# A vision-tower kernel on one Trainium2 core: pixels loaded by half patches, and three engines' orders rearranged

## What is computed

```python
# patches of 16x16 pixels, 3 channels: 36 patches per image, 768 numbers each
p = x.reshape(B, C, nh, PH, nw, PW).transpose(0, 2, 4, 3, 5, 1).reshape(B, 36, 768)
h = layernorm(p, ln1) @ W + b            # 768 -> 192
h = layernorm(h, ln2)
h = concat([cls, h], axis=1) + pos       # 37 tokens
# a linear state-space layer, h + attn(norm(h)):
xn = gamma * h / rms;  xp = xn @ W_in.T + b_in       # 192 -> 384
xc = causal_conv(xp, conv_w)                          # 4 taps
ys = scan(h = sigA*h + sigB*x;  y = h . sigC)         # 16 states per channel, 37 steps
h  = h + ys @ W_out.T + b_out + residual
# h + ffn(norm(h)): gelu MLP 192 -> 768 -> 192 for 31 tokens, expert pairs and a gate for 6
```

## Time and profile before

| | |
|---|---|
| median of 3 runs | 98.13 us (97.84 to 98.38) |
| the profiled execution's own time | 99.03 us |
| its span | 97.3 us |
| PE busy | 85.5 us (88%), 579 matmuls |
| DVE busy | 60.9 us (63%) |
| POOL busy | 41.1 us (42%) |
| ACT busy | 38.7 us (40%) |
| DMA | 13.59 MB, mean 140 GB/s |

### The profile page before, as it was taken

How to read it: one execution, slowest core, us unless ns; L and a number is a source line. 1 busy time by engine, 2 the same in 40 slices (tenths; PEclk the granted TensorE clock), 3 DMA queues, 4 the chain that set the end, 5 groups by cost and what they waited for, 6 DMA issues and landing times.

```text
span 97.3 us, 1841 instructions
## 1 busy us (share of the span) xinstructions
PE 85.5 (88%) x579; PEld 71.0 (73%) x579; DVE 60.9 (63%) x209; ACT 38.7 (40%) x105; POOL 41.1 (42%) x112
## 2 busy tenths in 40 slices
PE   5997599999988978969999989969899999999940
PEld 5995399989966758757588889956577726888830
DVE  4659999547999999999976993573100307038410
ACT  0620957562345644104492053420964204870000
POOL 6525799998974230538746005353500400000000
PEclk9999999999999999999999999999999999999996
DMA  1999998497628994699999921010202100000211
GB/s 14 262 259 255 257 275 150 87 259 175 194 67 268 322 214 136 109 281 235 246 326 314 292 68 41 17 46 13 78 20 81 34 28 11 0 0 0 63 52 39
DMA packets 16294, 13.59 MB, mean 140 GB/s; under 512 B 5907, under 2 KB 14332, under 8 KB 16284
## 3 DMA queue, kind: packets, MB, share of 16 engines
q1 hardware_dynamic: 14860, 13.39, 52.0%
q10 hardware_dynamic: 1424, 0.08, 1.2%
HBM read 12.43 MB, written 1.04 MB: 138 GB/s over the span
## 4 chain that ended last, share of the span: by engine, by line
PE 55%; DVE 24%; DMA 7%; ACT 4%; ACTq 3%; issue 3%; DVEq 0%
PE ps L1184 50%; DMA ssm<-in_L_attn_C_dram 7%; DVE h L994 3%; DVE xT_area L1027 2%; DVE xs L1012 2%; DVE xT_area L1030 2%; PE ps L1208 2%; DVE st L1000 2%; DVE h L977 2%; DVE st L967 2%; ACT x4TT L654 2%; DVE xT_area L1036 1%; ACT xT_area L654 1%; DVE ag L969 1%; DVE Y L1036 1%
## 5 line engine op out<-in xcount | busy, mean ns | idle before, releaser
L1184 PE MATMUL ps<-W_area,xT_area 128*108 128x192 f32 (+2 forms) x72 | 13.7, 329 | 1.5 <-ACT xT_area L654 1.3
L1184 PEld LDWEIGHTS ps<-W_area,xT_area 128*108 128x108 f32 (+2 forms) x72 | 10.9, 170 | 2.3 <-issue 2.1
L1184 PE MATMUL ps<-W_sb,pixel_area 128*124 128x192 f32 x48 | 8.8, 332 | 0.0
L1184 PEld LDWEIGHTS ps<-W_sb,pixel_area 128*124 128x124 f32 x48 | 7.7, 187 | 1.2 <-issue 1.2
L1184 PE MATMUL ps<-WoutT,xT_area 128*108 128x192 f32 (+1 forms) x42 | 7.6, 328 | 1.0 <-DVE xT_area L1036 1.0
L1184 PEld LDWEIGHTS ps<-WoutT,xT_area 128*108 128x108 f32 (+1 forms) x42 | 6.8, 177 | 1.4 <-DVE xT_area L1036 1.4
L1184 PE MATMUL ps<-dM,WinT 128*128 128x216 f32 (+2 forms) x36 | 7.2, 335 | 0.0
L1184 PE MATMUL ps<-x4TT,W_sb 128*128 128x248 f32 x24 | 6.1, 387 | 1.1 <-ACT x4TT L654 1.1
L654 ACT ACTIVATE xT_area<-ps,ln_col 128x576 f32<-128x576 f32 (+1 forms) x6 | 4.9, 809 | 4.5 <-PE ps L1208 4.5
L1184 PEld LDWEIGHTS ps<-dM,WinT 128*128 128x128 f32 x36 | 5.8, 190 | 0.8 <-issue 0.8
L1184 PE MATMUL ps<-warm_sb 128*128 128x128 f32 x24 | 5.4, 412 | 1.1 <-DVE warm_sb L863 1.1
(11 more groups left out here) (212 smaller groups left out, 197.3 us busy)
## 6 DMA issues: line engine op xcount, KB each, us to landing
line_area<-in_L_ffn_A_W_dram SPq DMA_DIRECT2D x5, 576.0 KB, 9.4
A_sb<-in_L_ffn_A_W_dram SPq DMA_DIRECT2D x5, 384.0 KB, 4.3
pixel_area<-in_x_dram SPq DMA_DIRECT2D x6, 288.0 KB, 7.1
A1R<-in_L_ffn_A_W_dram SPq DMA_DIRECT2D x10, 96.0 KB, 3.6
W_area<-in_L_tok_W_dram SPq DMA_DIRECT2D x2, 288.0 KB, 5.6
W_sb<-in_L_ffn_moe_W_dram SPq DMA_DIRECT2D x1, 576.0 KB, 8.2
W_sb<-in_L_ffn_moe_W_dram SPq DMA_DIRECT2D x1, 384.0 KB, 5.9
W1R<-in_L_ffn_moe_W_dram SPq DMA_DIRECT2D x2, 192.0 KB, 5.7
```

The lines of the kernel that those rows point to most:

```text
L1184: return t.matmul(out_, lhsT, rhs, start=start, stop=stop, skip_group_check=True)
```

## The change

- SP: the first four pixel and W loads are now x of the upper half for channels 0, 1, 2, with W's first half behind the first; then x(0, 1), W's second half, x(1, 1), x(2, 1). `chunks` follows (halves outside, channels inside), so chunk i is another piece of pixels, and the statistics are 36 `bn_stats` of 128 pixels rather than 12 of 256 and 12 of 128.
- PE: `product` and `turn` in another order; only one of three W_out transposes is made early, the other two (into bank 5) behind `project_in_odd(0)`; `product(4, [4, 5])`, `product(5, [4, 5])`, `fold([4, 5])` behind `transform(0)`; the `Kk` transposes behind `transform_rest(0)`, the `Fk` matmuls behind `project_in_even(0)`, `project_in_odd(0)` behind these; the `ob` matmuls behind `transform(4)`; `turn_x4(1)` beside `turn_x4(0)`, into bank 5; the MLP's first step in parts (`up_first`, `up_rest`), with `turn_x4(4)` and `(5)` between them.
- ACT: the load of the square-root table behind `put_xT(2)`; the DMAs for gamma behind `put_xT(3)`; `put_xT(5)` ahead of the root of the variance; the W_out copies exchanged, the large one behind the `K2` copies; `put_x4T(1)` ahead of `put_P(4)`.
- POOL: `add_cls` ahead of `root2(5)`.

The diff, cut to its core:

```diff
-        chunks = [(c, hh) for c in range(NC) for hh in range(H2)]
+        chunks = [(c, hh) for hh in range(H2) for c in range(NC)]
...
             load_x(0, 0)
             load_W(0)
+            load_x(1, 0)
+            load_x(2, 0)
             load_x(0, 1)
             load_W(1)
-            load_x(1, 0)
             load_x(1, 1)
-            load_x(2, 0)
             load_x(2, 1)
...
+            add_cls()
             root2(5)
-            add_cls()
...
-            a_.activation(table_row[:, 1:2], ones[:, 0:1], ACT.Sqrt)
             put_xT(1)
-            act.dma_start(gcol[:, 0:1], gamma[0:DL].unsqueeze(1)).then_inc(l_gam, 16)
...
             line_up(2)
             put_xT(2)
+            a_.activation(table_row[:, 1:2], ones[:, 0:1], ACT.Sqrt)
...
             put_xT(3)
+            act.dma_start(gcol[:, 0:1], gamma[0:DL].unsqueeze(1)).then_inc(l_gam, 16)
...
             act.wait_ge(t_w, 3)
-            copy(WoutT[:, 0:2, :], ps[:, 6, 0:2 * D].rearrange("p (e d) -> p e d", e=2)).then_inc(wT_ready, 1)
+            copy(WoutT[:, 2, :], ps[:, 3, 0:D]).then_inc(wT_ready, 1)
             roots3(1)
-            act.wait_ge(t_w, 4)
-            copy(WoutT[:, 2, :], ps[:, 3, 0:D]).then_inc(wT_ready, 1)
...
+            act.wait_ge(t_w, 4)
+            copy(WoutT[:, 0:2, :], ps[:, 5, 0:2 * D].rearrange("p (e d) -> p e d", e=2)).then_inc(wT_ready, 1)
             roots3(3)
...
             put_x4T(0)
+            put_x4T(1)
             put_P(4)
-            put_x4T(1)
...
-            for c in range(2):
-                for hh in range(H2):
-                    dve.wait_ge(l_x[c][hh], 16)
+            for i, (c, hh) in enumerate(chunks):
+                dve.wait_ge(l_x[c][hh], 16)
                 for nw in range(NW):
-                    step(v.bn_stats(st1[:, nw, c, :], x_pix[:, c, :, nw, :]))
...
+                    k = step(v.bn_stats(st1[:, nw, i, :], x_pix[:, c, HB * hh:HB * (hh + 1), nw, :]))
...
+                if g == 4:
+                    pe.wait_ge(x4T_ready, 2)
...
             transform(0)
+            product(4, [4, 5])
+            product(5, [4, 5])
+            fold([4, 5])
+            transform(1)
+            transform_rest(0)
             pe.wait_ge(K_ready, 1)
...
             ins.then_inc(t_K, 1)
-            transform(1)
-            transform_rest(0)
+            project_in_even(0)
             pe.wait_ge(KT_ready, 1)
...
             ins.then_inc(t_Kh, 1)
-            project_in_pair(0)
+            project_in_odd(0)
+            pe.wait_ge(h_free, 4)
+            turn_Wout(0, 5, 0)
+            turn_Wout(1, 5, D).then_inc(t_w, 1)
             transform(2)
...
+                for b0, nb, n in ((B0[0], NBG[0] + NBG[2], 3), (B0[3], NBG[3], 4)):
+                    pe.wait_ge(x4T_ready, n)
```

More of the change, by code:

```diff
@@ L1429, in _ @@
             project_out(0)
-            project_in_pair(1)
+            project_in_even(1)
+            project_in_odd(1)
+            project_out(1)
+            transform(4)
             pe.wait_ge(u_ready, 2)
@@ L1435, in _ @@
             ins.then_inc(t_ob, 1)
-            project_out(1)
-            transform(4)
             invert(0)
@@ L1443, in _ @@
             invert(1)
-            project_in_pair(2)
+            project_in_even(2)
+            project_in_odd(2)
             project_out(3)
+            turn_x4(0)
+            turn_x4(1)
             invert(2)
-            turn_x4(0)
             project_out(4)
-            turn_x4(1)
             invert(3)
@@ L1455, in _, with up @@
             turn_x4(3)
-            def up(s, js, last):
+            def up(s, js):
                 for j in js:
```

72 lines of the change are left out of this document (36 added, 36 removed).

## The result

| | before | after |
|---|---|---|
| median of the executions, us | 97.98 (97.37 to 98.38, 4) | 103.91 (103.69 to 104.32, 4) |
| profiled execution, us | 99.03 | 103.93 |
| its span, us | 97.3 | 101.9 |
| its mean granted clock | 0.991 | 0.981 |

The ratio is 1.062, 95% interval 1.055 to 1.068: slower, and by 3.7 us more than the 100.2 that I forecast, outside the range.

The account below looks back on a forecast made before the run. Bound by a chain of waits: PE to 22.49 us, DVE to 47.18, PE to the end. End -0.3 plus middle +2.4 gave 2.1 us later, 99.03 to 101.1 profiled, 100.2 in medians; range 98.9 to 102.0.

Parts of the forecast that it names:

- the first stage: Start up to `center(0)`: reordered PE products and later table load bring the fold earlier, `center(0)` at 21.35 rather than 22.49.
- That cover is thin, 0.3 us: First stage: DVE done with F at 19.2, the transpose it needs next arriving at 19.5.
- The gain of 1.1: First stage: the fold at 20.45 against 21.58, so DVE's `center(0)` starts 1.1 us sooner.
- The rival on the clock: PE's pauses at 24.4 and 35.5 to 39.7 halve its clock, falling at 38: about 102; chance 0.07.
- The gamma rival: First stage: gamma DMAs land too late for `WinT`, adding 1 to 2.5 us, about 101.8; chance 0.12.
- The middle: `xs` of group 0 to `transform(5)`: `normed(3)` waits for ACT's root behind the `WoutT` copy; `transform(5)` 2.4 us later, at 49.6.
- the collision: Middle: a DVE instruction of 0.42 took 1.13 beside POOL's `u_rep`; 0.4 us taken back, between 0 and 0.7.
- PE's way through `ob`: Middle: `put_P(1)` stands behind `ob` on ACT, so `invert(0)` waits; this path too puts `transform(5)` at 49.6.
- The spectrum itself is no worse: Middle: PE ends the spectrum at 34.5, ACT's copy at 35.5, under the 37.2 when `multiply(0)` wants it.
- The end: Behind `transform(5)`: 0.3 lost at `project_out(4)`, 0.6 regained around the MLP's first step, in all 0.3 us gained.

Follow-up runs that it names:

- e2: Kernel after the change, with GpSimd made to wait for F before its addition and reduction; median 103.83 us, ratio to before 1.056.
- e5: Kernel before with only the new pixel order, its loads and statistics, plus GpSimd's wait for F; 98.48 us, ratio 1.0054.
- e14: e2 with PE's pauses filled at three places by products of a constant tile, results unused; 101.42 us, ratio 1.034.
- e17: e2 with the filter's transposes and products back early and six filling products ahead of `transform(0)`; 100.09 us, ratio 1.023.
- e18: e17 with `roots3(3)` also ahead of WoutT's copy on ACT; 97.73 us, ratio 0.998.
- e7: Kernel before with the first stage of after, GpSimd's wait for F, and gamma's transfers behind the second chunk's copy; 98.25 us, ratio 1.0004.
- e3: Kernel after, with GpSimd's wait for F and the large `WoutT` copy moved behind `roots3(3)` on ACT; 102.44 us, ratio 1.041.
- e9: Kernel after, with GpSimd's wait for F, `roots3(3)` ahead of the filter's and WoutT's copies, and gamma's transfers early; median 102.41 us.
- e12: Kernel before with only the change's PE, ACT and GpSimd orders between `fold([2, 3])` and `project_out(3)`; 102.34 us, ratio 1.042.
- e13: Kernel after with PE's pauses filled by products of a constant tile, without GpSimd's wait; readable executions 102.21, 102.29, 102.34, 103.51 us.
- e15: e10 with the filter's transposes, products and copies early, as before the change; 97.30 us, ratio 0.990.
- e10: e9 with `roots3(5)` and `put_P(1)` ahead of the copy of `ob` on ACT; median 101.52 us.
- e11: e7 with the end of the kernel after; 98.65 us, ratio 1.003.

## Why the prediction was wrong

**The step that failed is the first stage's**, "DVE is done with F 0.8 later than 18.36, at 19.2", with "That cover is thin, 0.3 us". The statistics, PE's part and even the start of F were right within 0.1. What I left out is that F's own time depends on what GpSimd does beside it. I had the rows for it. In the trace of before (start, length) GpSimd's addition and reduction stand at 18.82 to 23.24, and I let F run until 19.2:

```profile
18.82 0.58 POOL L547 TENSOR_TENSOR posb<-posb,ln2b_bc 108x192 f32<-108x192 f32 x1
19.36 3.88 POOL L554 TENSOR_TENSOR powr_area<-powr_area 128x888 f32<-128x888 f32 x3
```

And the earlier trace rows show one DVE instruction of two SBUF inputs taking 1133 ns beside a POOL one instead of 417. I used that pattern for `add_cls` and did not ask it of the instruction that I had just moved by 0.8 us. F took 2.3 us more and was done at 21.55, not at 19.2; `center(0)` came at 23.38 where I had 21.35. The Trainium skill (SBUF — State Buffer, section SBUF: two separate sides) says that DVE and GpSimd share one port pair by an exclusive lock, held for the whole instruction, and that the loser blocks. The trace agrees in the main: the product with two SBUF inputs took 2.63 us instead of 0.22 to 0.30, while the two of `ms1T`, with one input in PSUM, took 0.25 and 0.21 us beside the same reduction. But the product let two GpSimd instructions by, not one. e2 and e5 show that the order of the two engines decides.

The gain of 1.1 was itself too large. With F repaired and no fall, `center(0)` came 14.1 behind the first product and `xs(0)` 18.6 to 19.0 (e2, e14, e17, e18), forecast 13.8 and 18.2: against 19.31 before, 0.3 to 0.7. With the old middle and end nothing of that reached the time (e7, 98.25).

**The rival on the clock came true as well.** I gave 0.07 to a fall, at 38. It fell at 23 to 26 in the profiled execution, behind a pause that F had made, and in three of the four executions it fell somewhere; in the traces of e3, e9 and e12 it fell at 39 to 42, near the place that I had named. Its size: e13 against after, some 1.6 us by the medians of the readable executions, 1.5% by the ratios. In the after kernel itself the one execution without a fall (clock 0.999) took 103.69, only 0.2 less than the median; so one of four speaks against this size. It has no trace, and the arrival of the first pixels, which moves the first product between 6.78 and 7.76 in the traces, can hide much of a fall's price in a single execution. What weighs more are e13 and e14, and the 34 executions of the unfilled kernels. I had seen the pauses (1.9 at 24.4, two at 35.5 to 39.7; in after 0.77, 1.28 and 1.39, and the 1.65 that I had not seen) and held them harmless because no trace had shown a fall inside the kernel; but no trace before had such pauses either, the longest there was 1.02 in this stretch. The Trainium skill's rule that an idle stretch puts the array back to half clock (TensorE: Matmul & The Clock Gate, What's actually happening) was the better guide than the absence of a row. The traces agree in part only: 1.65 us idle was followed by 0.50 in after, 1.73 was not in e2 and e15.

**The gamma rival** was hidden. The first transfer went out at 15.04, 0.02 us behind the end of the table load, when a copy, a line-up and `put_xT(3)` ahead of it had not begun, the last at 15.97. So ACT ran three instructions ahead and not the five for which I had 14.3. They landed at 21.37, when the fold was late anyhow. With F repaired (e2) `WinT` waits for them until 22.12, and `center(0)` to `xs(0)` takes 4.92 instead of 4.32 in e7. But the early place costs as much at the fold.

**The middle was right, and for the reason given**: 10.73 to `normed(3)` where I had 10.8, released by ACT's root behind the `WoutT` copy; 23.73 to `transform(5)` where I had 23.9. e12 puts 3.4 to 3.9 us on it in the time (101.37 and 101.80 at full clock, before 97.93). The 23.9 is in part luck: I had DVE, with 0.4 of the collision back, and PE's way through `ob` arrive together. The collision gave back 0.7 (1133 to 419 ns) and `multiply(0)` lost nothing to it, but PE's way, with `put_P(1)` behind `ob`, was the later of the two and hid that. But "The spectrum itself is no worse" held only behind the root's delay: with the root moved away (e9, e10) the filter's copies held `multiply(0)` at 9.75 instead of 7.50. A cover that is itself the loss is no cover. **The end**: 0.3 forecast, 0.33 measured.

Together: F and its pause 1.7 against before in `xs(0)`, the fall's 0.6 to 0.9 within it; the middle 3.4; the end -0.3; that is 4.8, against 4.6 between the spans and 0.16 for the earlier first product. Not settled: how the 0.6 to 0.9 of the first stage and the 1.6 of e13 divide over single falls, and where e11's three falls lie.

## What to carry to other kernels

When an edit shifts an instruction by less than a microsecond, look at what the engine that shares its memory port runs in the new place: its length there is another one. Judge an order by the longest pause that it leaves on PE as well as by its path, and put useful or even idle products into the pauses that a new order opens: here that alone gave 1.6 us (e13) and 2.4 (e14) in the medians, 1.5% and 2.2% in the ratios. Two late steps one behind the other must be moved together; here each alone showed about a third or less of what both are worth on the path (0.79 and 1.13 of 3.56).
